# The expert-key stage of a two-layer attention and feed-forward kernel: order of its PSUM traffic, and smaller parts for the split expert weights

## The chip, the cores and the metric
One Trainium2 chip, one core. The metric is the device time in microseconds of one execution of the whole program. All times below are microseconds (us) unless marked ns.

## The reference, cut to what matters
Four sub-layers on x of 4 sequences, 512 tokens, 256 channels, each added to x after a layer norm:

1. cross attention, 16 heads of 16 channels, with a time bias of -0.1 |t - t'|;
2. a dense feed-forward of 1024 channels plus product-key experts;
3. cross attention with relu on q, k and v, no bias;
4. eight experts of 512 channels with gelu, two chosen per token.

The change lies in the second (the "expert-key stage"), and in how the weights of the fourth are prepared during the first:

```python
q = einsum('btd,ed->bte', h, W_q); sim = einsum('pbthn,hkpn->pbthk', q, keys)   # 4 heads, 2 halves, 64 keys
sx, sy = top_k(sim, 8)
scores, pk = top_k(sx[:, None] + sy[None, :], 8)            # 8 of 64 pairs per head
w = silu(einsum('btd,bthkd->bthk', h, down_embed[indices]) * softmax(scores))
experts_states = einsum('bthk,bthkd->btd', w, up_embed[indices])
dense = silu(h @ W_up.T) @ W_down.T                          # 256 -> 1024 -> 256
```

## The kernel before, in words
Each engine has its own program, and semaphores order them. PSUM is one tile `ps` of 8 banks of 128 x 512 floats. Three parts matter.

**Attention 0** (0 to about 375 us) runs 64 units U (4 sequences x 4 head groups x 4 key blocks). In a unit TensorE makes four scores for the row maxima (L1002, VectorE reduces them at L1335), four scores by key (L1016), and the value products of the unit before (L1033); ScalarE takes the exp (L773); GpSimd multiplies the near-diagonal part (`near_bias`, L611) before the values may use it. Maxima of a head group are turned (L1050), copied (L1346) and carried by SyncE from `m_sb` into `sq` (`load_max`, L443), where the first scores by key of the group (units 48, 52, 56, 60 for the last sequence) wait for them. In units 3 and 19 GpSimd also does a layer norm (L558, then L568). Between near parts GpSimd splits each of the 8 experts' weights of sub-layer 4 into a high and a low part: `split_high` (L584), `split_low` (L590), `split_out` (L596, which stores them to HBM and asks for the raw weights of the expert after next, L603 and L604). Expert e's three parts run in units 5 + 7e, 6 + 7e and 7 + 7e. SyncE's program has, after its work for unit 56, `late_weights` (L483): it waits until all split weights are stored, then loads 4.9 MB of weights for the expert-key stage. After the last unit it queues the zeroing of 22 MB of `expert_rows` (L511).

**The expert-key stage** (375 to 793 us) works on 16 blocks n of 128 tokens, software-pipelined over steps s. The order of each engine's work in a step is written out by hand. Per block: `turn_norm` and `x_high`/`x_low` (once for two blocks: normed x turned to channels, in a high and a low part), `similarity` (L1115 with `wret`), `sim_copy`, `top8` on VectorE (L1558 to L1576, with L1560 and L1573 on SBUF), `turn_sim` (L1153), `turned_high` (L810) and `turned_low` (L1546), `hidden` (L1115 with `sk`: 1024 products of x with all experts, PSUM banks 0 and 1), and for each of 4 heads h: `logits` (L1174, 128 x 1024), `expand` (exp, L820), `mask` (L1584, keeps what is above the threshold), `times_hidden` (L1593), `weight_silu` (L835, in the next step). `norms8` (L1598 to L1603) makes the softmax sums, `clamped_pairs` (L635, L638, GpSimd) and `clamped_silu` (L840) a special expert. GpSimd's `add_heads` (L646) adds the four heads' 128 x 1024 weights. Three steps after its logits the block's summed weights are turned (`turn_weights`, L1181), copied, and multiplied with the up embeddings (`add_experts`, L1188). The dense feed-forward runs beside it: `ff_up` (L1115 with `ff1s`), `ff_silu`, `ff_down` (L1210). `add_pair` (L1611 to L1622) adds the results of two blocks to x. The copies of the front bank all go through `front_copy` (L791).

PSUM in this stage: banks 0 and 1 for `hidden`; banks 2 to 5 are two pairs, used in turn (`ring_free`) by a block's turned similarities and its four logits; bank 6 (`FRONT`) is used in the order of `front_order()` by x turned, similarities, summed weights turned, and the feed-forward in two halves; bank 7 sums the output. ScalarE's exp and silu are in different tables, so a step has two table loads.

The heads' weights live in buffers `wide`, of which head h has `KEEP[h]`: (3, 2, 2, 3).

**Attention 1** and the experts of sub-layer 4 follow (793 us to the end). Its q weights are scaled by `SCALE` on VectorE ahead of the expert-key stage (L1632).

## Time and profile before
| | us |
|---|---|
| median of 3 runs (1317.18 to 1319.8) | 1319.05 |
| the profiled execution | 1312.35 |
| its span, first to last instruction | 1310.5 |
| attention 0, to about | 375 |
| expert-key stage, its first logits to its last pair added | 397.2 to 793.1 |

The profile is of one execution. Busy time counts what an engine computes; instructions that only wait, branch or issue a DMA are not in it. "PE" is TensorE's matmul, "PEld" its weight load, "DVE" VectorE, "ACT" ScalarE, "POOL" GpSimd, "SPq" the DMA queue of SyncE. "[3.61 <-POOL pt L611]" behind a row means that the engine stood idle 3.61 us before it and that the named work of GpSimd ended the wait. Matmul ends are modelled and overlap, so a matmul row's length holds some latency at its end; GpSimd's spans are rough.

### The profile page before, as it was taken

Reading aid. Unit: us, or ns where it says so; the run is one execution under the profiler, and the core shown is the slowest. Engines: PE = TensorE matmul, PEld = TensorE weight load, DVE = VectorE, ACT = ScalarE, POOL = GpSimd, SP = SyncE. Lnnn points to the kernel's source line nnn. Section 1 sums busy time; section 2 is a strip of 40 time slices with the busy share of each in tenths; the row PEclk is TensorE's granted clock in tenths of the full one; section 3 lists DMA queues with packets and bytes.
Section 4 is the critical chain, followed back from the end, with each engine's and each line's share of the span. In section 5 each row is a group of like instructions: output and inputs, shape, how many; then the busy total and the mean of one; then the engine's idle time right before and its main releaser. Section 6 shows DMA issues by size and latency. Waiting matters only on the chain.

```text
span 1310.5 us, 16623 instructions
## 1 busy us (share of the span) xinstructions
PE 1060.7 (81%) x5420; PEld 653.2 (50%) x5420; DVE 809.9 (62%) x1941; ACT 661.0 (50%) x886; POOL 442.3 (34%) x342
## 2 busy tenths in 40 slices
PE   5797988988356788888888776999998985399992
PEld 3332333433134677767777664333333432288881
DVE  2755757677048878978888402677777773344443
ACT  2044645555344667566675632266656574155551
POOL 1327565566230434234343331011422143222220
PEclk9567989989679899999999988699988797599996
DMA  8836656651899800000000007436444334422226
GB/s 233 194 104 194 202 173 174 208 161 66 299 236 234 179 1 1 1 1 1 1 1 2 1 1 168 129 90 185 106 135 123 91 123 180 161 70 70 71 70 192
DMA packets 77801, 151.68 MB, mean 116 GB/s; under 512 B 8234, under 2 KB 48300, under 8 KB 76182
## 3 DMA queue, kind: packets, MB, share of 16 engines
q1 hardware_dynamic: 67446, 107.72, 31.8%
q0 software_dynamic: 9168, 42.12, 9.2%
q8 instruction: 46, 0.75, 0.3%
q10 hardware_dynamic: 1104, 0.79, 0.2%
q14 instruction: 37, 0.30, 0.1%
HBM read 73.88 MB, written 76.25 MB: 115 GB/s over the span
## 4 chain that ended last, share of the span: by engine, by line
PE 55%; DVE 12%; ACT 12%; issue 9%; POOL 6%; DMA 4%; SPq 1%; ACTq 0%; POOLq 0%; DVEq 0%
PE ps L1115 14%; PE ps L1033 6%; PE ps L1002 6%; DVE negmax L1335 6%; PE ps L981 6%; PE ps L1188 4%; PE ps L1016 3%; PE ps L1174 3%; PE ps L990 3%; PE ps L1210 2%; ACT moe_w L835 2%; POOL pt L611 2%; ACT pt L835 1%; POOL wst L590 1%; PE ps L1286 1%
## 5 line engine op out<-in xcount | busy, mean ns | idle before, releaser
L1335 DVE TENSOR_REDUCE negmax<-ps 128x1 f32<-128x512 f32 x512 | 320.9, 682 | 75.9 <-PE ps L1002 75.3
L773 ACT ACTIVATE pt<-ps 128x1024 f32<-128x1024 f32 x256 | 255.5, 1025 | 170.0 <-PE ps L1016 169.3
L1002 PE MATMUL ps<-sk,sq 56*128 56x512 f32 x512 | 174.6, 481 | 44.9 <-DVE negmax L1335 20.2
L1033 PE MATMUL ps<-pt,v_aug 128*32 128x512 f32 x1024 | 149.9, 660 | 19.7 <-POOL pt L611 18.7
L1016 PE MATMUL ps<-sq,sk 57*128 57x512 f32 x512 | 133.1, 511 | 21.0 <-DMA sq<-m_sb 19.8
L1002 PEld LDWEIGHTS ps<-sk,sq 56*128 56x128 f32 x512 | 78.2, 210 | 112.3 <-DVE negmax L1335 73.9
L611 POOL TENSOR_TENSOR pt<-pt,near 128x512 f32<-128x512 f32 x64 | 81.5, 1273 | 141.6 <-ACT pt L773 141.5
L1016 PEld LDWEIGHTS ps<-sq,sk 57*128 57x128 f32 x512 | 52.8, 201 | 121.8 <-issue 71.9
L686 POOL TENSOR_TENSOR x_tok<-x_tok,on 128x256 f32<-128x256 f32 x16 | 11.6, 725 | 228.5 <-DVE on L1355 228.5
L1174 PE MATMUL ps<-sel,hl 128*128 128x512 f32 x256 | 73.3, 420 | 6.7 <-DVE pt L1584 6.7
L708 POOL DMA_INDIRECT expert_out<-yo,dest x39 | 38.2, 979 | 117.3 <-ACT yo L921 89.3
L1115 PE MATMUL ps<-wexp,ghl 128*128 x468 | 67.2, 292 | 1.6 <-DVE ghl L1683 1.5
L1115 PE MATMUL ps<-wexp,xhl 128*128 x234 | 65.0, 414 | 1.5 <-DVE xhl L1679 1.5
L1683 DVE TENSOR_TENSOR ghl<-ps,ghl 128x512 fp32r<-128x512 f32 x39 | 27.0, 691 | 60.7 <-ACT ghl L914 60.7
L1210 PE MATMUL ps<-wff,on 128*128 128x256 f32 x256 | 63.6, 393 | 0.0
L635 POOL TENSOR_TENSOR wdown_e<-exm,ex 128x256 f32<-128x256 f32 x16 | 10.0, 626 | 158.6 <-DVEq L1605 158.6
L1188 PE MATMUL ps<-wup_e,xn 128*128 128x256 f32 x256 | 63.5, 385 | 0.0
L1115 PEld LDWEIGHTS ps<-wexp,ghl 128*128 128x128 f32 x468 | 58.9, 188 | 6.8 <-issue 2.2
L820 ACT ACTIVATE moe_w<-ps,negm 128x1024 f32<-128x1024 f32 x30 | 33.4, 1112 | 55.0 <-PE ps L1174 54.9
L1174 PEld LDWEIGHTS ps<-sel,hl 128*128 128x128 f32 x256 | 48.9, 193 | 18.3 <-DVE pt L1584 8.4
L1188 PEld LDWEIGHTS ps<-wup_e,xn 128*128 128x128 f32 x256 | 49.8, 195 | 8.3
L1033 PEld LDWEIGHTS ps<-pt,v_aug 128*32 128x32 f32 x1024 | 20.7, 111 | 61.3 <-issue 33.6
(251 smaller groups left out, 1996.6 us busy)
## 6 DMA issues: line engine op xcount, KB each, us to landing
expert_rows<-zero SPq DMA_DIRECT2D x3, 5586.0 KB, 58.2
qk_rows<-hl SPq DMA_DIRECT2D x32, 512.0 KB, 3.3
expert_weights_split<-wst POOLq DMA_DIRECT2D x8, 2048.0 KB, 8.6
sq<-qk_rows SPq DMA_DIRECT2D x64, 192.0 KB, 4.6
sk<-qk_rows SPq DMA_DIRECT2D x64, 192.0 KB, 5.3
qk_rows<-hl SPq DMA_DIRECT2D x32, 256.0 KB, 3.8
moe_w<-in_w POOLq DMA_DIRECT2D x16, 512.0 KB, 9.6
wexp<-expert_weights_split POOLq DMA_DIRECT2D x16, 512.0 KB, 5.0
```

Source lines behind the costliest of these rows:

```text
L611: pool.tensor_tensor(probs, probs, near[:].unsqueeze(1).broadcast_to([P, HG, P]), ALU.mult).then_inc(s_near, 1)
L773: act.activation(pt[:, 4 * (U % 2) + 2 * half:4 * (U % 2) + 2 * half + 2, :], ps[:, 2 + 2 * half:4 + 2 * half, :], ACT.Exp, scale=(BIAS, 1 ...
L835: act.activation(weight(n, h), weight(n, h), ACT.Silu, scale=rz[:, n % RING, h:h + 1]).then_inc(s_w4, 1)
L981: ins = pe.matmul(dst, w[L][:, part, i * P:(i + 1) * P], src[:, part, :], start=(part == 0), stop=(part == 1))
L1002: pe.matmul(ps[:, jbank(job), :], sq[r, pair, t * P:(t + 1) * P], sk[r, pair, :], start=True, stop=True).then_inc(s_job, 1)
L1016: ins = pe.matmul(ps[:, 2 + 2 * half + s, :], sk[r, pair, c * P:(c + 1) * P], sq[r, pair, :], start=True, stop=True)
L1033: ins = pe.matmul(ps[32 * j:32 * j + 32, OBANK, :], v_aug[:, b % 2, c, HG * g + j, :], pt[:, 4 * (U % 2) + j, :], start=(c == 0), stop=(c ...
L1115: ins = pe.matmul(dst, lhs(i), rhs(j), start=(first and i == j == 0), stop=(last and i == 1))
L1174: ins = pe.matmul(dst[:, j, :], turned[n % 2][:, i, h * P:(h + 1) * P], sel[:, NX * YK * j:NX * YK * (j + 1)], start=(i == 0), stop=(i == 1))
L1188: ins = pe.matmul(ps[:, YBANK, (n % 2) * D:(n % 2 + 1) * D], accT[:, c * P:(c + 1) * P], wup_e[:, c, :], start=False, stop=True, skip_grou ...
L1210: ins = pe.matmul(ps[:, YBANK, t * D:(t + 1) * D], ffh[:, 512 * i + 2 * P * r + P * t:512 * i + 2 * P * r + P * (t + 1)], wff2[:, f, :], s ...
L1335: dve.tensor_reduce(negmax[:, n % 2, col:col + 1], src, AX, ALU.max, negate=True).then_inc(s_jd, 1)
```

## The change
Attention 0:
- Expert e's split now has four parts in units 3 + 6e to 6 + 6e: high, low of the first half, low of the second half, out. `late_weights` stands after unit 53 instead of 56.

Expert-key stage:
- The turned similarities go through the front bank, and `front_order()` has them (`"T"`); the feed-forward goes through the bank pairs, all four of its 128-channel parts at once, in an order written down by `ring_order()`: the four logits of step s, then the feed-forward of block s - 2. `ff_silu` is one instruction of 128 x 1024.
- TensorE: `similarity(s + 2)` moves from the end of the step to between the third logits and the second part of `add_experts`; `turn_norm` to after the fourth logits; `ff_up` and then `turn_sim` close the step.
- ScalarE: `sim_copy` goes between the exps of heads 2 and 3, `x_high` behind them; the silus of heads 3 and 2, then the feed-forward's silu and `turned_high`, then the silus of heads 0 and 1.
- GpSimd: in step s it waits for the first mask of block s, then adds the heads of block s - 2 (before: of s - 1, without that wait), in the order 2, 0, 1, and only then does `clamped_pairs(s)`. Head 1 gets a third buffer (in `wff1`'s space).
- VectorE: `x_low` goes one step earlier, to between the products of heads 2 and 3.
- Start: both turns of x come before the first similarities. The scaling of the q weights of attention 1 is dropped, and `SCALE` is given to the exp there.

```diff
-RING, KEEP = 3, (3, 2, 2, 3)
+RING, KEEP = 3, (3, 3, 2, 3)
+def ring_order():
+    order = []
+    for s in range(NTL + 2):
+        if s < NTL:
+            order += [("S", s, h) for h in range(RH)]
+        if s >= 2:
+            order.append(("ff", s - 2, 0))
+    return order
@@ sync
-                    if L == 0 and U == 56:
+                    if L == 0 and U == 53:
                         late_weights()
@@ gpsimd
-                e, part = divmod(U - 5, 7)
-                if 0 <= e < ME and part < 3:
-                    (split_high, split_low, split_out)[part](e)
+                e, part = divmod(U - 3, 6)
+                if 0 <= e < ME:
+                    if part == 0:
+                        split_high(e)
+                    if part in (1, 2):
+                        split_low(e, part - 1)
+                    if part == 3:
+                        split_out(e)
-            for s in range(NTL + 1):
+            for s in range(NTL + 2):
+                if s < NTL:
+                    pool.wait_ge(s_pm, RH * s + 1)
+                if s >= 2:
+                    add_heads(s - 2)
                 if s < NTL:
                     clamped_pairs(s)
-                if s >= 1:
-                    add_heads(s - 1)
@@ scalar, one step
                     small_exp(s)
                     expand(s, 2)
-                    expand(s, 3)
-                if 0 <= s - 2 < NTL:
-                    ff_silu(s - 2, 0)
-                if s + 1 < NTL:
-                    turned_high(s + 1)
-                if 0 <= s - 2 < NTL:
-                    ff_silu(s - 2, 1)
-                if 0 <= s - 1 < NTL:
-                    weight_silu(s - 1, 3)
-                    weight_silu(s - 1, 1)
                 if s + 2 < NTL:
                     sim_copy(s + 2)
+                if s < NTL:
+                    expand(s, 3)
                 if s % 2 and (s + 3) // 2 < NTL // 2:
                     x_high((s + 3) // 2)
                 if 0 <= s - 1 < NTL:
+                    weight_silu(s - 1, 3)
                     weight_silu(s - 1, 2)
+                if 0 <= s - 2 < NTL:
+                    ff_silu(s - 2)
+                if s + 1 < NTL:
+                    turned_high(s + 1)
+                if 0 <= s - 1 < NTL:
                     weight_silu(s - 1, 0)
+                    weight_silu(s - 1, 1)
                     clamped_silu(s - 1)
@@ tensor, one step
                     logits(n, 2)
+                if s + 2 < NTL:
+                    similarity(s + 2)
...
                     logits(n, 3)
+                if s % 2 and (s + 3) // 2 < NTL // 2:
+                    turn_norm((s + 3) // 2)
                 if 0 <= y < NTL:
                     add_experts(y, range(6, EC))
                 if 0 <= s - 2 < NTL:
-                    ff_up(s - 2, 0)
+                    ff_up(s - 2)
                 if s + 1 < NTL:
                     turn_sim(s + 1)
-                if 0 <= s - 2 < NTL:
-                    ff_up(s - 2, 1)
-                if s + 2 < NTL:
-                    similarity(s + 2)
-                if s % 2 and (s + 3) // 2 < NTL // 2:
-                    turn_norm((s + 3) // 2)
+            def pair_free(item):
+                i = pairs[item]
+                if i >= 2:
+                    kind, m, h = order4[i - 2]
+                    pe.wait_ge(*((s_fs, m + 1) if kind == "ff" else (s_pm, RH * m + h + 1)))
+                return ps[:, 2 + 2 * (i % 2):4 + 2 * (i % 2), :]
@@ vector, start
-            dve.wait_ge(s_late, 16 * 8)
-            own(dve.tensor_scalar(wq[1][:], wq[1][:], SCALE, None, ALU.mult))
```

## Rows read from the trace of the kernel before

**Rows 1.** The page's first part: busy time, share of the span, instructions.
```profile
PE 1060.7 (81%) x5420; PEld 653.2 (50%) x5420; DVE 809.9 (62%) x1941; ACT 661.0 (50%) x886; POOL 442.3 (34%) x342
```
**Rows 2.** Windows: stretch, length, then PE, PEld, DVE, ACT, POOL busy, clock, DMA, GB/s.
```profile
334.80:353.40 18.60, 0.04 (x6) 0.02 (x2) 0.00 (x0) 0.00 (x0) 1.15 (x1) 0.59 0.86 301
...
443.80:740.00 296.20, 254.85 (x1317) 213.34 (x1317) 240.47 (x569) 193.81 (x248) 110.25 (x65) 0.99 0.03 6
740.00:793.10 53.10, 39.07 (x202) 33.13 (x200) 9.36 (x18) 22.97 (x31) 15.88 (x9) 0.94 0.07 8
...
559.45:606.04 46.59, 39.96 (x208) 33.42 (x209) 38.82 (x95) 30.52 (x40) 17.00 (x10) 1.00 0.00 1
```
**Rows 3.** Timeline of SyncE's DMA queue: start, length, what is issued.
```profile
298.46 16.23 SPq L443 DMA_DIRECT2D sq<-m_sb  x4
336.41 0.91 SPq L483 DMA_DIRECT2D wff<-in_ff  x2
...
345.40 2.14 SPq L443 DMA_DIRECT2D sq<-m_sb  x2
```
**Rows 4.** The page's DMA issues: count, KB each, median us to landing.
```profile
expert_weights_split<-wst POOLq DMA_DIRECT2D x8, 2048.0 KB, 8.6
```
**Rows 5.** Timeline of TensorE around the hole.
```profile
325.83 0.73 PE L1016 MATMUL ps<-sq,sk 57*128 57x512 f32 x4
...
353.38 1.22 PE L1016 MATMUL ps<-sq,sk 57*128 57x512 f32 x4 [18.56 <-DMA sq<-m_sb]
```
**Rows 6.** Timeline of ScalarE and TensorE over one step of the expert-key stage.
```profile
585.69 1.14 ACT L835 ACTIVATE w_first<-w_first,rz 128x1024 f32<-128x1024 f32 x1
586.73 1.14 ACT L835 ACTIVATE moe_w<-moe_w,rz 128x1024 f32<-128x1024 f32 x1
...
590.94 1.28 ACT L820 ACT_TABLE_LOAD   x1
...
592.23 1.11 ACT L820 ACTIVATE pt<-ps,negm 128x1024 f32<-128x1024 f32 x1
...
594.24 0.60 ACT L791 ACTIVATE xn<-ps 128x512 f32<-128x512 f32 x1
...
594.89 0.66 PE L1181 MATMUL ps<-ident,moe_w 128*128 128x128 f32 x4 [0.67 <-ACT xn L791]
...
600.45 1.27 PE L1174 MATMUL ps<-sel,hl 128*128 128x512 f32 x4
...
601.76 1.12 ACT L820 ACTIVATE moe_w<-ps,negm 128x1024 f32<-128x1024 f32 x1 [1.11 <-PE ps L1174]
```
**Rows 7.** Timeline of GpSimd in attention 0: norm, high part, near part, low part.
```profile
94.62 4.83 POOL L558 TENSOR_SCALAR xn<-x_tok,mv,rstd 128x256 f32<-128x256 f32 x4
...
110.07 1.89 POOL L584 CAST wst<-moe_w 128x2048 fp32r<-128x2048 f32 x1 [2.58 <-DMA moe_w<-in_w]
...
294.70 1.29 POOL L611 TENSOR_TENSOR pt<-pt,near 128x512 f32<-128x512 f32 x1
...
322.78 4.56 POOL L590 TENSOR_TENSOR wst<-moe_w,wst 128x2048 fp32r<-128x2048 f32 x1
```
**Rows 8.** Waits of TensorE, 40 to 375: total, times, longest.
```profile
PE ps L1033 <- POOL pt L611: 18.7, 8, 4.9
```
**Rows 9.** Timeline of GpSimd and VectorE at the stage's start.
```profile
374.75 4.50 POOL L625 TENSOR_TENSOR sk<-wdown_e,sk 128x2048 fp32r<-128x2048 f32 x1 [8.66 <-ACT sk L853]
...
375.75 3.78 DVE L1632 TENSOR_SCALAR wq<-wq 128x512 f32<-128x512 f32 x1
```
**Rows 10.** Groups by line, 559.45 to 606.04: busy us, mean ns, idle before.
```profile
L1560 DVE TENSOR_TENSOR wdown_e<-sxy 128x256 f32<-128x256 f32 x2 | 3.1, 1528 | 0.1
L1573 DVE TENSOR_TENSOR wdown_e<-wdown_e,v 128x256 f32<-128x256 f32 x2 | 3.0, 1500 | 0.1
```
**Rows 11.** One line's instructions over the run: ns shortest, median, longest.
```profile
L1560 DVE TENSOR_TENSOR wdown_e<-sxy x16: 425/1036/2039, 389.0 to 705.4; 128x256 f32<-128x256 f32 x16
```
**Rows 12.** Timeline of VectorE and GpSimd: a mask beside a sum.
```profile
731.25 1.28 DVE L1584 SCALAR_TENSOR_TENSOR pt<-ps,thr,pt 128x1024 f32<-128x1024 f32 x1 [4.88 <-ACT pt L820]
731.33 2.36 POOL L646 TENSOR_TENSOR w_first<-w_first,pt 128x1024 f32<-128x1024 f32 x1
```

More of the change, by code:

```diff
@@ L171, in front_order @@
 def front_order():
-    order = [("xt", 0, 0), ("sim", 0, 0), ("sim", 1, 0), ("xt", 1, 0)]
+    order = [("xt", 0, 0), ("xt", 1, 0), ("sim", 0, 0), ("sim", 1, 0), ("T", 0, 0)]
     for s in range(NTL + 3):
@@ L176, in front_order @@
             order += [("at", s - 3, 0), ("at", s - 3, 1)]
-        if 0 <= s - 2 < NTL:
-            order += [("ff", s - 2, 0), ("ff", s - 2, 1)]
         if s + 2 < NTL:
@@ L182, in front_order @@
             order.append(("xt", (s + 3) // 2, 0))
+        if s + 1 < NTL:
+            order.append(("T", s + 1, 0))
+    return order
[6 more added lines that the diff above has]
+            order.append(("ff", s - 2, 0))
     return order
@@ L365, in build @@
         order6 = front_order()
+        pairs = {item: n for n, item in enumerate(ring_order())}
+        order4 = ring_order()
+        pair_of = lambda item: ps[:, 2 + 2 * (pairs[item] % 2):4 + 2 * (pairs[item] % 2), :].rearrange("p a t -> p (a t)")
         s_x = [sem(f"x_in{b}") for b in range(B)]
@@ L513, in _ @@
             sp.wait_ge(s_hd, NTL)
-            sp.wait_ge(s_front, front["ff", NTL - 1, 1] + 1)
+            sp.wait_ge(s_f, NTL)
             const_rows(1)
@@ L640, in add_heads @@
             def add_heads(n):
-                for i, h in enumerate((1, 2, 0)):
+                for i, h in enumerate((2, 0, 1)):
                     pool.wait_ge(s_w4, RH * n + i + 2)
@@ L794, in x_high @@
                 if p >= 4:
-                    act.wait_ge(s_front, front["ff", 2 * (p - 4) + 1, 1] + 1)
+                    act.wait_ge(s_f, 2 * (p - 4) + 2)
                     act.wait_ge(s_hd, 2 * (p - 4) + 2)
@@ L800, in sim_copy @@
                 if n >= 2:
-                    act.wait_ge(s_T, n - 1)
+                    act.wait_ge(s_front, front["T", n - 2, 0] + 1)
                     act.wait_ge(s_top, n - 1)
@@ L805, in turned_high @@
             def turned_high(n):
-                act.wait_ge(s_T, n + 1)
                 if n >= 2:
                     act.wait_ge(s_S, RH * (n - 1))
-                r = 2 + 2 * (5 * n % 2)
-                act.copy(turned[n % 2][:, 0], ps[:, r, :]).then_inc(s_th, 1)
+                front_copy(turned[n % 2][:, 0], ("T", n, 0))
             def expand(n, h):
-                i = 1 + 5 * n + h
                 act.wait_ge(s_S, RH * n + h + 1)
@@ L1220, in _ @@
             turn_norm(0)
+            turn_norm(1)
             similarity(0)
+            similarity(1)
             turn_sim(0)
-            similarity(1)
-            turn_norm(1)
             for s in range(NTL + 3):
@@ L1543, in turned_low @@
             def turned_low(n):
-                dve.wait_ge(s_th, n + 1)
-                r = 2 + 2 * (5 * n % 2)
-                dve.tensor_tensor(turned[n % 2][:, 1], ps[:, r, :], turned[n % 2][:, 0].bitcast(F32), ALU.subtract).then_inc(s_tl, 1)
+                dve.wait_ge(s_fe, front["T", n, 0] + 1)
+                dve.tensor_tensor(turned[n % 2][:, 1], ps[:, FRONT, :], turned[n % 2][:, 0].bitcast(F32), ALU.subtract).then_inc(s_tl, 1)
             def top8(n):
@@ L1666, in _ @@
                     times_hidden(n, 2)
+                if s % 2 and (s + 3) // 2 < NTL // 2:
+                    x_low((s + 3) // 2)
+                if n < NTL:
                     times_hidden(n, 3)
```

86 lines of the change are left out of this document (43 added, 43 removed).

## The prediction
> **What bounds the kernel now.** The page's first line says that TensorE is busy 81% of the span and every other engine less [rows 1]; an average over stages doesn't say what a stage waits for, so I read the windows view next [rows 2]. In 334.8 to 353.4 no engine computes: 18.6 us are lost. From 443.8 to 740.0, the body of the expert-key stage, TensorE is busy 86% and VectorE 81%: neither is full, so an order of work holds it. The chain of waits repeats there every two steps; the window of two steps is 46.59 us, one step 23.3.
>
> The hole: the timeline of SyncE's queue [rows 3] shows the loads of the last group of row maxima (L443, `sq<-m_sb`) at 345.40, behind the late weights (L483) that start at 336.41, because SyncE waits there for the last split expert weights to be stored; that store has a median of 8.6 from issue to landing [rows 4]. TensorE [rows 5] waits 18.56 for those maxima, until 353.38.
>
> The body: I follow one step through the timeline [rows 6], from its last logits to the next ones. ScalarE turns it around: exp at 601.76, silus, a table load at 590.94 in the step before, the two exps, the copy at 594.24; TensorE has it from 594.89 to the last logits at 600.45. ScalarE also waits twice within it, because the feed-forward goes through the one front bank in two halves with a silu each (the first ends near 606.0).
>
> **Part 1, expert weights.** Expert 7 is now sent in unit 48, not 56. In [rows 7] the near multiply of unit 48 starts at 294.70 and ends at 296. With 8.6 for the store the late weights can start at 304.6. Their issue lasts 9.0 (336.41 to 345.40 [rows 3]), to 313.6. The next maxima are asked for at about 313.4 in the trace (they are the second pair of the row 298.46, which is 16.23 long), so SyncE is free when it is asked. Behind the weights they land some 17 after the weights' start (336.41 to 353.38), at 321.6. TensorE wants them in unit 56, at 325.83 [rows 5]: 4 us are left. The last group, asked for near 330, finds an empty queue. **18.6 saved**; if the store or the queue takes some us more, a new wait of up to 6 takes its place: 13 to 20 (above 18.6, because TensorE starts again cold after the hole: clock 0.59 in it [rows 2]).
>
> GpSimd's low half of 4.56 [rows 7] becomes two of 2.28. TensorE takes about 4.3 for a unit (from the norm of unit 3 at 94.6 to the hole at 334.8, 56 units) and the near multiply 1.3, so a piece of 2.3 fits beside it and one of 4.5 does not. TensorE waited for this multiply 18.7 in eight waits [rows 8]. What is late next: in unit 3 the norm (4.83), the bias add (2.3), the loads (3.3), their landing (2.58) and the high part (1.89) now stand in one row, 14.9, instead of 7.2 and 7.7 with two multiplies between. I work out that the values of unit 9 come some 4 later; in unit 19 the norm is rid of the high part beside it (2 to 3 won), and the low parts give about 4. Net **2 saved**, -4 to 7.
>
> **Part 2, start of the stage.** The scaling of `wq` on VectorE becomes a constant of ScalarE's exp, which costs nothing. Its row is 3.78 long [rows 9] for 512 columns and it ended 0.3 after GpSimd's 4.50, which began at 374.75: it was held by GpSimd. What is late next may be the norm behind it, held till the same 379.3; then 0.5 is won, and 3.6 if the norm is not held. Against this, a second turn, copy, low part and norm go ahead of the first similarity, about 3 on the path, while the first copy of similarities no longer stands behind the square root, 1. I take **1 saved**, -1 to 4.
>
> The Trainium skill (SBUF — State Buffer, section Who interferes with whom) says that a DVE `tensor_scalar` can enter a mode that contends with GpSimd, and that an instruction with two SBUF inputs contends with a GpSimd one that reads SBUF. The 3.78 agrees with such a lock. By that rule the norm, too, is held, and this part gives under 1.
>
> **Part 3, the steps.** The new circle from [rows 6], counted from the issue of a step's last logits:
> - to the start of its exp 1.31 (600.45 to 601.76), exp 1.12, table load 1.28;
> - two weight silus at a pitch of 1.04 (585.69, 586.73), 2.08; the feed-forward silu, now one of the same size, 1.04 (its 24 matmuls end about 5.1 after the start, ScalarE comes at 5.8, so both waits of before are gone); the copy of the turned similarities 0.5;
> - two more silus 2.08, the clamped one 0.61, table load 1.29, two exps 2.01 (592.23 to 594.24), copy and turn-around 0.65. Together 13.97.
> - TensorE from there: 5.56 as now (594.89 to 600.45) and the similarity put in between, six matmuls, 1.4: 6.96.
>
> A step takes 20.9. Odd steps add a copy (0.5) and a turn (0.4): 21.8.
>
> Beside it lies VectorE, 19.4 a step now [rows 2]. The sums now run after the first mask, 3 x 2.4 = 7.2. Before, they ran beside the top-8 block, where L1560 and L1573 average 1.53 and 1.50 [rows 10]; L1560's shortest is 0.43 and its longest 2.04 [rows 11]. Laid out from start to start the block loses 2.2 in one step and 3.4 in the next, so VectorE needs 19.4 - 2.8 = 16.6. Does the new company hold the masks? At 731.25 a mask takes 1.28 with a GpSimd sum beside it from 731.33 [rows 12], as without: no. It may hold the small products of `norms8`, which read SBUF twice like L1573: in odd steps the masks come late (first mask ends 17.4 after the circle's start, behind `add_pair`, 2.6, and the norm, 0.8), the sums end at 24.9, and `norms8`, due at 23.5, waits 1.4. Last mask, two products and low part pass it on to the next hidden block, which has 1.1 to spare: 0.3 reaches the circle. The new wait of exp 2 for the first sum (its buffer has two turns): in even steps the first mask ends at 13.7, the sum at 16.1, and the exp is due at 18.6, so it is free; in odd ones it is 0.8 late, where the mask behind it has that slack. The held sums are wanted a step after they end, and `clamped_pairs`, moved behind them, has its reader a step away.
>
> Mean (20.9 + 22.1) / 2 = 21.5 against 23.3: 1.8 x 12.7 steps (296.2 / 23.3) = **22.9 saved**. TensorE's own floor is 39.96 / 2 = 20.0, so the circle still binds. Bounds: 22.5 if VectorE's path decides (10 saved), 20.9 throughout (30).
>
> Before 443.8 one top-8 block loses its company: **2 saved**, -2 to 4. The tail, 53.1 from 740.0 [rows 2]: laid out the same way it is 48.6 (the last feed-forward blocks in one piece each, but two weight silus queue behind a feed-forward silu that waits for TensorE): **4.5 saved**, 0 to 8.
>
> **Sum.** 18.6 + 2 + 1 + 22.9 + 2 + 4.5 = 51.0. The profiled execution took 1312.35 (span 1310.5 and 1.85 around it), so its like would take 1261.35. The median of the three runs is 1319.05, 6.7 above it; I take the saving from the median: **1268.0 us**.
>
> **Rivals.**
> A. *The circle is not what binds the body.* VectorE's chain (turned low, pair add, top-8, masks) or the pair banks hold a step at 23. For it: VectorE at 81%, and only 1.1 spare in odd steps; against it: the 2.8 it gets back. The stage gives 4 instead of 22.9: 1286.9. Chance 0.16.
> B. *The maxima are caught again.* 5 MB stand ahead of a small load that TensorE wants 4 us after. Were the last store 13 later, 9 of the hole come back: 1277. For it: 17 us of queue. Against it: the margin of about a unit. Chance 0.08.
> C. *Slower.* One mechanism: GpSimd's sums and the masks exclude each other. VectorE then needs 16.6 + 7.2 = 23.8, and with the waits for ScalarE that it can't avoid (about 2.6) a step takes 26.4: 3.1 x 12.7 = 39 lost against 28.1 won elsewhere: 1330. The whole is slower from a step of 25.5 on. Against it stands the mask at 731.25. Chance 0.04.
> D. *Better*: masks and sums keep clear, all steps take 20.9, the splits give their 7: 1255. Chance 0.12.
> E. *It does nothing*, other waits take all of it: 1319. Chance 0.03.
>
> **How the numbers follow.** The forecast's own case has 0.57. Its terms' bounds, added as squares, give 11 below and 16 above: 1257 to 1284. To leave out no more than 2 in 10 I reach towards A and D: 1251 to 1290. Faster by over 0.2% (2.6 us, about what can be told from no change): forecast, A, B and D, 0.93; same 0.03 (E); slower 0.04 (C).
>
> **What would show it.** No wait of many us for `m_sb` near 334, the late weights issued near 305; one longer hole in unit 3 on GpSimd's account; two steps in about 43 us, with no ScalarE wait between halves of a feed-forward; L1560 and L1573 at 0.43, masks still 1.28; `norms8` products stretched in odd steps. The forecast is wrong if two steps take over 45, or if the hole of part 1 only moves.

## The result and the profile after

| | before | after |
|---|---|---|
| median of the timed runs | 1318.32 us | 1263.27 us (1258.83 to 1268.79, 4 runs) |
| ratio, 95% interval | | 0.9585 (0.9562 to 0.9608) |
| span of the profiled execution | 1310.5 us | 1257.0 us |

The kernel is 55 us faster; 1268.0 was forecast and the time lies inside 1251 to 1290. In a second series of the changed kernel (below) two of six runs, 1358.07 and 3112.83 us, were disturbed and are left out. The page's first part, after, against [rows 1]: TensorE does the same 5420 matmuls, VectorE is busy 31.8 us less.

```profile
PE 1048.3 (83%) x5420; PEld 651.6 (52%) x5420; DVE 778.1 (62%) x1940; ACT 659.1 (52%) x870; POOL 443.4 (35%) x350
```

Where the 53.5 us between the two spans went is read from the same events in both traces: the first logits of the stage, those of step 3, the last logits of step 15, the last `add_pair`. Three rows of the timeline of before (TensorE, VectorE; its last logits are at 740.00, where a window of [rows 2] begins), and four of after:

```profile
397.18 1.97 PE L1174 MATMUL ps<-sel,hl 128*128 128x512 f32 x8
...
450.41 1.99 PE L1174 MATMUL ps<-sel,hl 128*128 128x512 f32 x8
...
793.06 0.69 DVE L1611 TENSOR_TENSOR x_tok<-ps,x_tok 128x512 f32<-128x512 f32 x1 [21.43 <-PE ps L1188]
```
```profile
373.26 1.98 PE L1198 MATMUL ps<-sel,hl 128*128 128x512 f32 x8
...
427.60 2.01 PE L1198 MATMUL ps<-sel,hl 128*128 128x512 f32 x8
...
691.88 1.28 PE L1198 MATMUL ps<-sel,hl 128*128 128x512 f32 x4
...
735.47 0.69 DVE L1631 TENSOR_TENSOR x_tok<-ps,x_tok 128x512 f32<-128x512 f32 x1 [19.43 <-PE ps L1212]
```

| stretch | before | after | saved | forecast |
|---|---|---|---|---|
| to the first logits (parts 1 and 2) | 397.18 | 373.26 | 23.9 | 21.6 |
| first logits to step 3 (ramp) | 53.23 | 54.34 | -1.1 | 2 |
| step 3 to the last logits (body) | 289.59 | 264.28 | 25.3 | 22.9 |
| last logits to the last pair (tail) | 53.06 | 43.59 | 9.5 | 4.5 |
| the rest of the kernel | 517.4 | 521.5 | -4.1 | 0 |

These are one trace each, and they scatter. A second trace of the changed kernel has 372.16, 59.47, 269.21, 43.36 and 522.0 in these rows: between two executions of the same kernel the ramp and the body each differ by 5 us, and the tail does not. TensorE's mean granted clock in the ramp was 0.91 in the first trace and 0.80 in the second.

The hole is gone. SyncE's queue of after, where [rows 3] showed the late weights at 336.41 and the last maxima at 345.40: the weights are issued at 299.42, and the maxima that units 56 and 60 want (L458) follow from 308.53.

```profile
299.42 0.91 SPq L498 DMA_DIRECT2D wff<-in_ff  x2
...
308.53 15.96 SPq L458 DMA_DIRECT2D sq<-m_sb  x4
```

The waits of TensorE from 40 to 375 (total, times, longest) now hold 1.8 us for `m_sb`. The waits for the near multiply, 18.7 in [rows 8], are not fewer:

```profile
PE ps L1053 <- POOL pt L626: 19.9, 9, 11.3
...
PE ps L1036 <- DMA sq<-m_sb: 1.8, 3, 1.1
```

The 11.3 is the wait for the near multiply that follows unit 3's long row. GpSimd's timeline there shows norm, bias, loads and high part in one row, 14.9 us from 92.14 to 107.02, before the near multiply that TensorE wants:

```profile
92.14 4.83 POOL L573 TENSOR_SCALAR xn<-x_tok,mv,rstd 128x256 f32<-128x256 f32 x4
97.05 2.34 POOL L583 TENSOR_TENSOR x_tok<-x_tok,bo_bc 128x1024 f32<-128x1024 f32 x1
...
105.16 1.89 POOL L599 CAST wst<-moe_w 128x2048 fp32r<-128x2048 f32 x1 [2.59 <-DMA moe_w<-in_w]
107.02 1.25 POOL L626 TENSOR_TENSOR pt<-pt,near 128x512 f32<-128x512 f32 x1
```

The body: the windows view of two steps, after (length, PE, PEld, DVE, ACT, POOL busy, clock). 46.59 of [rows 2] became 42.78, VectorE's busy time fell from 38.82 to 34.43:

```profile
546.70:589.48 42.78, 39.07 (x211) 33.47 (x209) 34.43 (x95) 30.32 (x37) 17.02 (x11) 1.00 0.00 1
```

ScalarE's timeline of one step, against [rows 6]. The step's last logits start at 546.70, those of the next at 567.48, 20.8 later. From the exp at 548.01 to the copy at 559.91 no row has a wait, and the feed-forward has a single silu (L850, 552.54) of one microsecond where two stood with a wait each:

```profile
548.01 1.12 ACT L841 ACTIVATE wff<-ps,negm 128x1024 f32<-128x1024 f32 x1 [1.53 <-PE ps L1198]
549.14 1.28 ACT L856 ACT_TABLE_LOAD   x1
550.44 1.16 ACT L856 ACTIVATE w_first<-w_first,rz 128x1024 f32<-128x1024 f32 x1
...
552.54 1.00 ACT L850 ACTIVATE on<-ps 128x1024 f32<-128x1024 f32 x1
553.44 0.58 ACT L813 ACTIVATE hl<-ps 128x512 fp32r<-128x512 f32 x1
...
557.90 2.12 ACT L841 ACTIVATE pt<-ps,negm 128x1024 f32<-128x1024 f32 x2
559.91 0.60 ACT L813 ACTIVATE xn<-ps 128x512 f32<-128x512 f32 x1
```

VectorE's lines over the whole run (ns shortest, median, longest). The first product of the top-8 block (L1582) is at 424 where [rows 11] had 1036, the masks (L1605) stay at 1283, and the small product of `norms8` (L1619) has a new longest of 1750:

```profile
L1582 DVE TENSOR_TENSOR wdown_e<-sxy x16: 424/424/1072, 365.8 to 662.1; 128x256 f32<-128x256 f32 x16
...
L1605 DVE SCALAR_TENSOR_TENSOR moe_w<-ps,thr,moe_w x26: 1273/1283/1285, 379.2 to 692.1; 128x1024 f32<-128x1024 f32 x26
...
L1619 DVE TENSOR_TENSOR exm<-ex,ixg x16: 179/182/1750, 381.7 to 694.5; 128x32 f32<-128x32 f32 x16
```

### The profile page after: what moved, and what is told of

Same layout as the page of the kernel before. It is cut to its first block, busy times and chain, and to the rows that moved or that the text cites. A ratio compares the mean times of both kernels' runs of the same rounds, so it can differ in the third digit from the quotient of the medians.

```text
span 1257.0 us, 16614 instructions
## 1 busy us (share of the span) xinstructions
PE 1048.3 (83%) x5420; PEld 651.6 (52%) x5420; DVE 778.1 (62%) x1940; ACT 659.1 (52%) x870; POOL 443.4 (35%) x350
## 4 chain that ended last, share of the span: by engine, by line
PE 55%; DVE 20%; ACT 7%; issue 7%; POOL 5%; DMA 4%; SPq 1%; ACTq 0%; DVEq 0%; POOLq 0%
PE ps L1135 14%; PE ps L1053 7%; PE ps L1022 7%; DVE negmax L1358 6%; PE ps L1001 6%; PE ps L1036 4%; PE ps L1010 3%; PE ps L1235 3%; PE ps L1198 3%; PE ps L1212 2%; DMA sq<-m_sb 2%; PE ps L1062 1%; PE ps L1309 1%; DVE moe_w L1613 1%; POOL pt L626 1%
## 5 line engine op out<-in xcount | busy, mean ns | idle before, releaser
L795 ACT ACTIVATE pt<-ps 128x1024 f32<-128x1024 f32 x256 | 255.8, 1025 | 157.0 <-PE ps L1036 150.3
L1022 PE MATMUL ps<-sk,sq 56*128 56x512 f32 x512 | 175.0, 478 | 48.3 <-DVE negmax L1358 21.2
L1053 PE MATMUL ps<-pt,v_aug 128*32 128x512 f32 x1024 | 146.9, 648 | 20.8 <-POOL pt L626 19.9
L708 POOL TENSOR_TENSOR x_tok<-x_tok,on 128x256 f32<-128x256 f32 x16 | 11.6, 725 | 234.0 <-DVE on L1378 234.0
L666 POOL TENSOR_TENSOR w_first<-w_first,moe_w 128x1024 f32<-128x1024 f32 x16 | 38.1, 2379 | 108.1 <-DVE pt L1605 107.3
L1605 DVE SCALAR_TENSOR_TENSOR moe_w<-ps,thr,moe_w 128x1024 f32<-128x1024 f32 x26 | 33.3, 1280 | 37.7 <-ACT moe_w L841 37.6
L841 ACT ACTIVATE moe_w<-ps,negm 128x1024 f32<-128x1024 f32 x26 | 28.9, 1112 | 49.1 <-PE ps L1198 27.9
```

The lines of the kernel that those rows point to most:

```text
L666: pool.tensor_tensor(weight(n, 3), weight(n, 3), weight(n, h), ALU.add).then_inc(s_sum, 1)
L795: act.activation(pt[:, 4 * (U % 2) + 2 * half:4 * (U % 2) + 2 * half + 2, :], ps[:, 2 + 2 * half:4 + 2 * half, :], ACT.Exp, scale=(BIAS, S ...
L1022: pe.matmul(ps[:, jbank(job), :], sq[r, pair, t * P:(t + 1) * P], sk[r, pair, :], start=True, stop=True).then_inc(s_job, 1)
L1053: ins = pe.matmul(ps[32 * j:32 * j + 32, OBANK, :], v_aug[:, b % 2, c, HG * g + j, :], pt[:, 4 * (U % 2) + j, :], start=(c == 0), stop=(c ...
```

## Experiments

The time from the last logits of step 3 to those of step 14, eleven steps, is the measure of the body below: 255.4 before (460.8 to 716.2) and 234.0 in this trace of after (438.5 to 672.5). A step counts as odd when it is the one in which the next tokens' normalised low part is made (20.8 us from 546.70 to 567.48 is an even one, 22.0 to 589.48 an odd one).

### Part 1 alone

```diff
-                    if L == 0 and U == 56:
+                    if L == 0 and U == 53:
...
-                e, part = divmod(U - 5, 7)
-                if 0 <= e < ME and part < 3:
-                    (split_high, split_low, split_out)[part](e)
+                e, part = divmod(U - 3, 6)
...
+                    if part in (1, 2):
+                        split_low(e, part - 1)
...
```


> The kernel before with part 1 alone: the split of the expert weights in four parts from unit 3 on, every 6 units, and the late weights after unit 53. The stage marks of the two profiles put 22.3 us of the gain ahead of the end of attention 0. If that is part 1's, this kernel takes 1318.3 - 22.3 = 1296, and two steps of the expert-key stage stay at 46.6. If part of the gain in attention 0 came from elsewhere (the run's clock), it takes 1299 to 1305.

Measured: 1291.36 us (1285.72 to 1298.86) against 1317.36; ratio 0.9812 (0.9745 to 0.9879), a saving of 24.8 with some 9 to either side. By the marks of its trace the first logits come at 373.65 instead of 397.18, 23.5 earlier; the body takes 255.4, as before, and two steps take 46.59. So the marks add up: part 1 brings its 22 to 24 and nothing behind it. The steadiest mark is the time from the first scores by key of unit 47 to those of unit 63: 73.2 in the traces of the kernel before and of the one with the held sums alone (below), 51.1 here and 51.0 in the first trace of the changed kernel, so 22.1 saved.

### The late weights where they were

```diff
-                    if L == 0 and U == 53:
+                    if L == 0 and U == 56:
```


> The changed kernel with the late weights back after unit 56. Theory 1 (the hole came from the late store of expert 7, not from the place of the loads): the store is done by about 299, the weights are then issued after the third pair of maxima, near 310, and have landed before the last pair is wanted: 1263 to 1265. Theory 2 (the place counts): the last pair of maxima stands behind 5 MB again, asked for at 323 and landed near 329 where TensorE wants it at 330: 1266 to 1275.

Measured: 1263.36 us; ratio 0.9586 (0.9535 to 0.9638), the same as the changed kernel. SyncE's queue in it: the maxima of units 52 and 56 are issued ahead of the weights, and the weights follow at once, without a wait for the store. The last maxima (unit 60's) are issued at 321.90, behind the weights, and TensorE does not wait for them either.

```profile
293.38 14.43 SPq L458 DMA_DIRECT2D sq<-m_sb  x4
307.92 0.91 SPq L498 DMA_DIRECT2D wff<-in_ff  x2
```

With the early store the place of the weights in the queue makes no difference: what caught the maxima was the late store. The old pacing with the weights at unit 53 can't be tried: SyncE would wait there for a store of unit 56, whose scores need maxima loaded behind it.

### Splits one unit later

```diff
-                e, part = divmod(U - 3, 6)
+                e, part = divmod(U - 4, 6)
```


> The changed kernel with the split parts one unit later (unit 4 + 6e and on), so that the first high part, with its loads, doesn't stand in the unit of the norm. Theory: the wait of 11.3 for GpSimd near 108 falls to about 4 and a second of about 2 comes: 4 to 5 us faster than the changed kernel, 1259. Rival: TensorE makes up for it within some units anyway, or unit 19 (norm beside store and loads) takes it back: 1262 to 1264.

Measured: 1266.84 us; ratio 0.9612 (0.9561 to 0.9663): no gain. The long wait in unit 3 did shrink (the longest for a near multiply is 5.2 instead of 11.3), but at the other end rival B came true in small. SyncE's queue, then TensorE:

```profile
306.61 0.91 SPq L498 DMA_DIRECT2D wff<-in_ff  x2
```
```profile
323.22 0.50 PE L1036 MATMUL ps<-sq,sk 57*128 57x512 f32 x2 [3.24 <-DMA sq<-m_sb]
```

The weights wait for the last store, are issued 7.2 later than in the changed kernel, and stand in front of the maxima: TensorE waits 3.24 for them in unit 56. This also tells how much slack the changed kernel has: here the maxima are issued at 316.67 and used 6.55 later, there they are issued at 308.53 and used at 316.03, so about 0.9 us was left. The last logits of the first step come at 389.1, 9.8 later than in the changed kernel; 3.24 of this is that wait, 3.4 was there by unit 47 (288.65 against 285.29), which lies within what traces of the same pacing scatter by (283.5 to 289.8), and the rest was not taken apart. The expectation of 1259 was wrong since it looked at unit 3 alone.

### Held sums alone

```diff
-RING, KEEP = 3, (3, 2, 2, 3)
+RING, KEEP = 3, (3, 3, 2, 3)
...
-                for i, h in enumerate((1, 2, 0)):
+                for i, h in enumerate((2, 1, 0)):
...
-            for s in range(NTL + 1):
+            for s in range(NTL + 2):
+                if s < NTL:
+                    pool.wait_ge(s_pm, RH * s + 1)
+                if s >= 2:
+                    add_heads(s - 2)
                 if s < NTL:
                     clamped_pairs(s)
-                if s >= 1:
-                    add_heads(s - 1)
...
```


> The kernel before with the held sums alone: GpSimd waits for the first mask and adds the heads of block s - 2, in the order 2, 1, 0, with a third buffer for head 1. Theory 1 (the chain through ScalarE and TensorE binds, and it is as long as before): top-8 is freed of its company, and the time stays within 4 us of 1318. Theory 2 (VectorE's work binds): 2.8 a step are won, two steps take 41 to 43, the kernel 1284.

Measured: 1316.59 us; ratio 0.9997 (0.9971 to 1.0023). The top-8 product is at 424 (median) and VectorE is 5.5 us less busy in two steps than in [rows 2], but the two steps take the same 46.60:

```profile
549.50:596.10 46.60, 39.98 (x211) 33.43 (x209) 33.27 (x94) 30.54 (x40) 16.95 (x11) 1.00 0.00 1
```

The body takes 255.4 (456.4 to 711.8), to the tenth that of before. VectorE did not bind the body: rival A, as far as it names VectorE, is out for the kernel before.

### Everything but the held sums

```diff
-            for s in range(NTL + 2):
-                if s < NTL:
-                    pool.wait_ge(s_pm, RH * s + 1)
-                if s >= 2:
-                    add_heads(s - 2)
+            for s in range(NTL + 1):
                 if s < NTL:
                     clamped_pairs(s)
+                if s >= 1:
+                    add_heads(s - 1)
```


> The changed kernel with GpSimd's order of before: clamped pairs of step s, then the sums of block s - 1, no wait for the mask. Theory 1 (the sums' company lengthens the top-8 block, and in odd steps VectorE passes that on): the two SBUF tensor operations of top-8 go back to 1.5 on average, two steps go from 42.8 to 44 to 46, the kernel takes 1270 to 1282. Theory 2 (the chain through ScalarE alone binds, VectorE has room): two steps stay at 42.8, within 3 us of 1263.

Measured: 1273.65 us; ratio 0.9688 (0.9631 to 0.9745), 10 us more than the changed kernel. Two steps take 47.3, more than the 44 to 46 expected. Windows of two steps, and VectorE's lines (ns shortest, median, longest), where the product into `x_tok` takes 482 (median) in the changed kernel:

```profile
549.70:597.00 47.30, 41.15 (x211) 34.50 (x209) 39.72 (x95) 30.32 (x37) 17.06 (x10) 0.96 0.00 1
```
```profile
L1633 DVE SCALAR_TENSOR_TENSOR x_tok<-last_up,wc,x_tok x16: 478/2570/2600, 465.5 to 751.6; 128x256 f32<-128x256 f32 x16
...
L1580 DVE TENSOR_TENSOR wdown_e<-sxy x16: 424/1553/2161, 364.1 to 677.1; 128x256 f32<-128x256 f32 x16
```

One of two steps takes 21.3, the other (which the changed kernel does in 20.8) 26.0, and the body 251.9 (435.6 to 687.4). So neither half does much alone:

| body, 11 steps | sums as before | sums held |
|---|---|---|
| the other edits not made | 255.4 | 255.4 |
| the other edits made | 251.9 | 234.0 (238.9 in a second trace, below) |

The circle of ScalarE and TensorE hid VectorE's slowness; once it is shortened, VectorE's path with the stretched operations sets every second step, and the held sums remove that. Which of the other edits shortened the circle, and by how much each, no run takes apart: the order of TensorE and ScalarE, the traffic of the banks and the single silu were changed together.

### A copy more on ScalarE, a sum more on VectorE

Two kernels, each the changed one with one instruction of 128x512 more in each step from 3; its result is read by nobody.

```diff
+                    if s >= 3:
+                        act.activation(wff1[:, 1, 0:512], wff1[:, 1, 512:FF], ACT.Copy)
```


> The changed kernel with one more copy of 128 x 512 on ScalarE behind the fourth exp, in steps 3 to 15 (result unused). A copy costs ScalarE 0.5 from start to start. Theory 1 (ScalarE's chain binds): 0.5 in each even step and 0 to 0.5 in odd ones, where ScalarE waits up to 0.5 for the turned similarities: 3 to 6.5 us slower than the changed kernel, 1266 to 1270. Theory 2 (VectorE's chain binds both steps): within 1 us of 1263.


```diff
+                if 3 <= s < NTL:
+                    dve.tensor_tensor(wff1[:, 1, 0:512], wff1[:, 1, 512:FF], wff1[:, 1, 512:FF], ALU.add)
```


> The changed kernel with one more sum of 128 x 512 on VectorE ahead of top-8, in steps 3 to 15 (result unused), 0.6 from start to start. Theory 1 (ScalarE's chain binds even steps, VectorE's tail leaks into odd ones only): 0 in even and 0.6 in odd steps, 3 to 4 us slower, 1267. Theory 2 (VectorE's chain binds both steps): 0.6 in each, 8 us slower, 1271. Theory 3 (ScalarE's chain alone): 1263.

Measured: 1267.54 us, ratio 0.962 (0.956 to 0.968), for the copy; 1272.91 us, ratio 0.9659 (0.9604 to 0.9713), for the sum. By the last logits of each step in the traces, even steps are 21.3 with the copy and 20.8 to 21.2 with the sum: ScalarE's circle sets them, and the copy of 0.5 goes straight through. Odd steps from 5 on are 22.0 to 23.6 with the copy, as without it (22.0 to 23.7 in the two traces of the changed kernel), and 23.6 to 25.3 with the sum: VectorE's path sets those. The theory that ScalarE's chain sets all steps holds for the even ones alone. The sum was to cost 3 to 4 us and cost about 10: each of its odd steps is long, and the next rows show what else than the 0.6 of the sum lies in a long one.

### A third buffer for head 2

```diff
-RING, KEEP = 3, (3, 3, 2, 3)
+RING, KEEP = 3, (3, 3, 3, 3)
...
```


> The changed kernel with a third buffer for head 2, so that its exp no longer waits for GpSimd's first sum (0.8 in odd steps). Theory 1 (that wait is hidden: the norms' product waits for the third sum in any case): within 1 us of 1263. Theory 2 (the wait is on the path): 0.8 in six odd steps, 5 us faster, 1258.

Measured: 1264.44 us; ratio 0.9597 (0.9544 to 0.9649), no difference. The wait of exp 2 for the first sum (3.82 at 565.90 in the changed kernel) is gone and nothing moved: it was hidden. But in this trace two steps take 44.3, not 42.8, and one row shows why. TensorE at the end of an odd step, of the changed kernel and of this one, then windows of this one:

```profile
575.78 3.00 PE L1135 MATMUL ps<-sk,xs 128*128 128x512 f32 x12 [0.55 <-DVE w_first L1613]
```
```profile
577.13 4.56 PE L1135 MATMUL ps<-sk,xs 128*128 128x512 f32 x12 [0.55 <-DVE w_first L1613]
```
```profile
573.30:577.10 3.80, 1.60 (x13) 1.19 (x11) 3.69 (x4) 3.27 (x4) 0.91 (x2) 1.00 0.00 0
577.10:581.50 4.40, 4.37 (x12) 3.56 (x13) 4.08 (x26) 4.03 (x6) 0.00 (x0) 0.61 0.01 4
```

TensorE computes for 1.60 of 3.80 us, with waits of 1.69 and 0.55 between, the second for VectorE, and then the granted clock is 0.61 on average for 4.40 us (1.00 is 2.4 GHz, 0.5 is 1.2 GHz): the same 12 matmuls take 1.56 longer.

### The changed kernel again, with and without spare work for TensorE

> The changed kernel itself once more, as the reference for the two that follow. Two of its relatives (late56, three_bufs) showed two steps in 44.3 to 44.4 where the first trace of the changed kernel shows 42.8; the difference is one stretch of 12 matmuls in odd steps, 3.0 at a granted clock of 1.00 or 4.4 at 0.61. Theory 1 (chance decides it, the same kernel shows both): this trace has some steps of 22.0 and some of 23.5, and the runs spread over 1258 to 1269. Theory 2 (the first trace is the rule for this kernel): all odd steps but one at 22.0.


```diff
+                if s % 2 and 3 <= s and s + 1 < NTL:
+                    spare = pair_free(("S", s + 1, 0))
+                    for k in range(KC):
+                        products(spare[:, 0, :], lambda i: xst[s // 2 % 4][:, i, k, 0:P], lambda j: wret[:, j, k, :], k == 0, k == KC - 1)
```


> The changed kernel with six spare matmuls (128x512) in each odd step from 3, put into a free pair bank while TensorE waits there, before the similarities are turned; their result is overwritten unread. Theory 1 (TensorE's idle of 2.2 in 3.8 us is why its clock falls, and the slow 12 matmuls are the whole difference between steps of 22.0 and 23.5): all odd steps take 22.0, the 12 matmuls 3.0 at clock 1.00; against the changed kernel in the same series 0 to 7 us faster, by how many of its steps are slow, about 1258 to 1261. Theory 2 (the clock falls for other reasons, or the spare work is itself in the way): steps of 23.5 stay, 1263 or more.

Measured, in one series: 1261.67 us (median of four runs, 1258.69 to 1267.98), ratio 0.9585 (0.9547 to 0.9622), and 1259.45 us (1254.90 to 1262.52), ratio 0.9581 (0.9552 to 0.961), with the spare matmuls (six runs). The second trace of the changed kernel has two steps of 44.40 at a clock of 0.96, where the first has 42.78 at 1.00. With the spare work all odd steps from 5 on take 22.0 to 22.3 (two steps: 42.80 at 1.00), although TensorE is busy for 1.6 us more than in the first trace (40.69 against 39.07):

```profile
552.50:596.90 44.40, 40.68 (x211) 34.69 (x209) 34.54 (x95) 30.33 (x37) 17.15 (x11) 0.96 0.00 1
```
```profile
548.20:591.00 42.80, 40.69 (x217) 34.51 (x215) 34.50 (x95) 30.32 (x37) 17.06 (x11) 1.00 0.00 1
...
573.40:577.20 3.80, 3.24 (x19) 2.27 (x17) 3.76 (x4) 3.24 (x4) 0.96 (x2) 1.00 0.00 0
```

The traces show theory 1: the same kernel has both lengths of odd step, and filling the idle stretch (3.24 busy of 3.80 instead of 1.60) keeps the clock. The idle stretch is needed for the loss but is not enough for it: in the first trace it was there and the clock stayed. The two medians alone don't separate the kernels.

### `norms8` ahead of the masks

```diff
                 if n < NTL:
+                    norms8(n)
                     mask(n, 0)
                     mask(n, 1)
...
-                    norms8(n)
                     mask(n, 3)
```


> VectorE does the two small products of norms8 before the first two masks of a step, not after the third. Theory 1 (in odd steps VectorE's path sets the length: the product is held 1.4 to 2.1 by GpSimd's third sum, and TensorE's next 12 matmuls wait for the masks and products behind it): that product takes 0.18 in every step, the odd steps shrink from 22.0 or 23.5 to 21.3 (ScalarE's 20.8 and its extra copy of 0.5), the even ones stay at 20.8, TensorE no longer idles long enough to lose its clock; 1252 to 1259. Theory 2 (something else sets the odd step): 1262 to 1266 as before it, though the product is no longer held.

Measured: 1266.70 us; ratio 0.9634 (0.9599 to 0.967), no gain or a small loss. The mechanism is as theory 1 has it: the small product takes 180 to 183 ns in all 16 steps, TensorE's 12 matmuls 3.00, odd steps 21.6, and the body 233.6 against 238.9 in the reference of the same series. But for the first blocks and for every even block (whose masks lie at the end of an odd step) the exps that `norms8` reads are not done yet, and the masks behind `norms8` now wait for them, 2.15 in block 0 and 3.4 in block 10:

```profile
377.86 0.19 DVE L1618 TENSOR_REDUCE zz<-ex 128x4 f32<-128x32 f32 x1 [2.15 <-ACT ex L844]
...
589.75 0.19 DVE L1618 TENSOR_REDUCE zz<-ex 128x4 f32<-128x32 f32 x1 [3.41 <-ACT ex L844]
```

Even steps are 21.1 instead of 20.8 (this is in the 233.6). No such wait is in them: there `norms8` itself, about 0.9 from its first row to its last, now stands between the norm and the first mask. From the first logits to the last ones of step 3 it is 0.8 longer and from those of step 14 to the last pair 1.2, which is 2 of the 5.3 that the body gives. In this trace the other 3 are lost outside the stage, which starts 2.2 later and is followed by 0.9 more than in the reference; whether the median shows no gain for this reason is not shown.

### Together

```diff
-RING, KEEP = 3, (3, 3, 2, 3)
+RING, KEEP = 3, (3, 3, 3, 3)
...
+                    if n % 2 and n >= 3:
+                        norms8(n)
                     mask(n, 0)
...
-                    norms8(n)
+                    if n % 2 == 0 or n < 3:
+                        norms8(n)
                     mask(n, 3)
-                    times_hidden(n, 2)
                 if s % 2 and (s + 3) // 2 < NTL // 2:
                     x_low((s + 3) // 2)
                 if n < NTL:
+                    times_hidden(n, 2)
                     times_hidden(n, 3)
```


> What the last runs point to, together: the products of norms8 go before the first masks in odd steps from 3 alone (there the small exp they need is already done; in even steps it is not, and norms_up held the masks for it), the third buffer of head 2 as in three_bufs, and the low part of the normalised tokens one product earlier. Theory 1 (the odd steps hang on VectorE's path behind the held product, the even ones on ScalarE's circle): even steps 20.8 as in the changed kernel, odd ones 21.3 to 21.6 with the 12 matmuls at full clock, the ramp as in the changed kernel; against its 22.0 to 23.5 in six odd steps that is 3 to 13 less: 1252 to 1259. Theory 2 (what norms_up lost was not only the wait of the masks in even steps): 1262 or more.

Measured: 1252.25 us (1246.18 to 1257.68) against 1309.71; ratio 0.9551 (0.9516 to 0.9586). The body takes 231.5 (445.9 to 677.4) and two steps 42.40 at a clock of 1.00. Odd steps are 21.3, as expected; even ones are 21.1 where 20.8 was expected, since `norms8` stands ahead of the first mask there as in the run before:

```profile
552.00:594.40 42.40, 39.39 (x210) 33.34 (x209) 33.33 (x95) 30.32 (x37) 16.97 (x11) 1.00 0.01 1
```

Its ratio is 0.0034 below that of the changed kernel, 4.5 us, and the intervals overlap; the body in the trace is 2.5 and 7.4 shorter than in the two traces of the changed kernel. Part of its lower median is that the kernel before was quicker in this series too.

## Why the prediction was right, and where it was off

The mechanisms of the hole and of the even steps were right, and the body's size nearly so; in odd steps VectorE decides, not ScalarE. That the sum came within 5 us of the median is in part luck: in the table of stretches the five misses add up to 17 us without their signs and to 2.5 with them.

- *Part 1, the hole.* Right, mechanism and size. Store, late weights (estimated 304.6, issued 299.42), maxima in time: 18.6 of the 23.9; TensorE's longest wait for `m_sb` fell from 18.56 [rows 5] to 1.1. The weights were earlier than estimated for two reasons: unit 48's near multiply came 3.2 earlier (below), and they left 6.7 after the store's issue at 292.73, not 8.6. The margin was misread. The prediction has TensorE want the maxima of unit 56 at 325.83 [rows 5], landed at 321.6, with 4 us left; but that row is unit 57 (four scores by key to a unit, 512 in the two attentions), and unit 56 starts at this one, in the kernel before:

```profile
321.57 0.50 PE L1016 MATMUL ps<-sq,sk 57*128 57x512 f32 x2
```

  With the weights at 304.6 nothing would have been left. They came 5.2 earlier, unit 56 came 5.5 earlier too (316.03), and about 0.9 was left: no wait, but that was luck and not the margin laid out. With the splits one unit later it is used up.
- *Part 1, pacing.* The long row in unit 3 came as laid out (14.9), the longest wait for a near multiply rose from 4.9 to 11.3, and the sum of these waits from 18.7 to 19.9. The near multiply of unit 48, at 294.70 in [rows 7], is at 291.50, but these 3.2 are not the pacing's: the kernel with the held sums alone, which has the old pacing, has it at 291.27. What is steady lies behind unit 47. From there to unit 59 the old pacing takes 43.05 (43.06 with the held sums alone) and the new 40.54, 2.5 saved where I had 2, and from unit 59 to 63, where the hole was, 30.14 became 10.48. GpSimd's timeline:

```profile
291.50 1.27 POOL L626 TENSOR_TENSOR pt<-pt,near 128x512 f32<-128x512 f32 x1
292.73 0.61 POOL L611 DMA_DIRECT2D expert_weights_split<-wst  x1
```

- *Part 2.* The norm was held, as allowed for: two pieces took 1.36 (the first alone 1.04) where the run's median of one is 0.41.

```profile
350.13 4.51 POOL L645 TENSOR_TENSOR sk<-wdown_e,sk 128x2048 fp32r<-128x2048 f32 x1 [9.95 <-ACT sk L874]
```
```profile
353.75 1.36 DVE L1559 TENSOR_SCALAR oT<-x_tok,mv,rstd 128x256 f32<-128x256 f32 x2
```

  The first piece ended about when GpSimd's 4.51 did (354.6). How much part 2 gave is not shown: the first logits come at 373.65 with part 1 alone and at 373.26 with all, 0.4 apart, and from the first scores of unit 63 to them it is 36.3 with part 1 alone, 37.0 and 34.0 in the two traces of the changed kernel. By the rule of the Trainium skill (SBUF — State Buffer, section Who interferes with whom) a `tensor_scalar` can be held in this way; this row agrees.
- *The circle in even steps.* 20.9 forecast, 20.8 measured, and a copy more on ScalarE lengthens them by its 0.5: this step of the working is shown.
- *Odd steps.* 22.1 forecast, 22.0 or 23.5 measured. I had ScalarE's two more operations setting them, with VectorE 0.3 over; the two extra-work runs show that it is VectorE. Its rows: the `norms8` product is held by GpSimd's third sum, as forecast (1.4), and everything behind it comes late, until TensorE's 12 matmuls wait for the last product.

```profile
569.38 0.17 DVE L1618 TENSOR_REDUCE zz<-ex 128x4 f32<-128x32 f32 x1
569.47 1.43 DVE L1619 TENSOR_TENSOR exm<-ex,ixg 128x32 f32<-128x32 f32 x1
...
573.82 0.68 DVE L1563 TENSOR_TENSOR hl<-ps,hl 128x512 fp32r<-128x512 f32 x1
574.42 1.22 DVE L1613 TENSOR_TENSOR w_first<-ps,w_first 128x1024 f32<-128x1024 f32 x1
```

  The rule of the Trainium skill (SBUF — State Buffer, section Who interferes with whom) on instructions with two SBUF inputs agrees with this row, and with the masks, which have one input in PSUM and were not held. What I did not think of is the clock: 1.5 of the step in some executions. It is why the body of the same kernel is 4.9 longer in its second trace.
- *Body.* 25.3 measured against 22.9. Over steps 3 to 14 the mean step went from 255.4 / 11 = 23.2 to 234.0 / 11 = 21.3 in this trace and 238.9 / 11 = 21.7 in the second, against 23.3 and 21.5 forecast. The gain per step was off by 0.1 to 0.3. What the table has beyond the 22.9 comes mostly from the last step: up to the last logits of step 15 it takes 19.4 in both traces where it took 23.8 before, and the forecast had priced all steps alike.
- *Held sums.* I forecast no cost for the masks beside a sum: right (1283 before and after). I gave the relief of VectorE no price of its own, because the circle binds; on its own that is right (0.9997), but taken away from the changed kernel it costs 10 us. `add_pair` takes 2.7 in the first trace (554.66 to 557.33) where my layout had 2.6.
- *Ramp.* 2 saved forecast, 1.1 lost, and 6.2 lost in the second trace. This term was guessed from one top-8 block. Its last step shows what it left out: it takes 24.7 (21.9 before), the `norms8` product is held there too (1.45), and TensorE waits for VectorE's last product and then does its 12 matmuls in 4.58 instead of 3.00:

```profile
423.18 4.58 PE L1135 MATMUL ps<-sk,xs 128*128 128x512 f32 x12 [3.23 <-DVE wff L1613]
```

  The rest was not taken apart.
- *Tail.* The term that was sized worst: 4.5 forecast, 9.5 measured. The last three steps in blocks, from one first feed-forward matmul to the next: before 741.78, 760.27, 778.83 and the end at 793.06; after 693.67, 707.31, 723.49 and the end at 735.47. That is 4.9, 2.4 and 2.3 saved. I had let the silus behind the feed-forward silu eat about half of this. ScalarE's rows show it mostly in the second block (710.57: two silus, 711.49, stand between it and the copy at 715.68, for which TensorE waits 2.67); in the first, two silus went ahead of the feed-forward silu, while TensorE made its 24 matmuls, and TensorE waits 1.06 for the copy at 701.20.

```profile
697.72 1.00 ACT L850 ACTIVATE on<-ps 128x1024 f32<-128x1024 f32 x1
...
701.20 0.58 ACT L813 ACTIVATE xn<-ps 128x512 f32<-128x512 f32 x1
...
710.57 1.02 ACT L850 ACTIVATE on<-ps 128x1024 f32<-128x1024 f32 x1 [5.32 <-PE ps L1135]
711.49 2.17 ACT L856 ACTIVATE pt<-pt,rz 128x1024 f32<-128x1024 f32 x2
...
715.68 0.58 ACT L813 ACTIVATE xn<-ps 128x512 f32<-128x512 f32 x1
```
- *The rest.* 4.1 lost, with nothing changed in it but the scale given to the exp of attention 1 (the 256 exps of both attentions have a mean of 1025 ns before and after). From the last pair to the end the kernel with held sums alone takes 521.9 and the one with part 1 alone 519.9, and of those built on the changed kernel the one with the spare matmuls takes 517.5 and the last one 515.1: the loss lies within the scatter between executions.
- *Rivals.* A is out for the kernel before, as far as VectorE goes, and half true after: VectorE's path sets the odd steps, at 22 to 23.5, not 23 for all. The pair banks, its other half, had no run of their own; they are used five times a step before and after, and the steps shrank. B did not happen, but does one unit further on. C did not happen (masks at 1283). D's 20.9 in every step is nearly reached by the last experiment (21.1 and 21.3).

## What to carry to other kernels

Two engines' paths of nearly the same length hide each other's faults: relieving the one that doesn't bind gave nothing by itself, and 10 us once the other was shortened, so an edit's worth has to be read from the kernel it will live in. When a step is rebuilt, follow each of its instructions to who is beside it on GpSimd, and check that what an operation reads is ready before it is moved ahead of others. A slack in a queue is part of the design, and the row that it is read from decides it: 4 us on paper were 0.9 in the trace, and moving the last store by one unit used them up. Compare a difference of a few microseconds between two traces with that between two traces of one kernel before giving it a cause.

## What was not expected of the hardware

The granted clock of TensorE fell within the body, which looks full: after 1.60 us of work in 3.80 the next 12 matmuls ran at 0.61 for 4.40 us and took 4.56 instead of 3.00. In four traces all odd steps from 5 to 11 are long by this (23.4 to 23.7), in the first trace of the changed kernel one is, for the same instructions; with 3.24 of 3.80 busy every odd step from 5 on stayed at 22.0 to 22.3. In the ramp, too, the clock decides microseconds: the same stretch took 54.34 at 0.91 and 59.47 at 0.80. What sets which of the two an execution gets is open. GpSimd's sums held a VectorE product of 128x32 values for 1.42 to 2.12 us instead of 0.18, and the product into `x_tok`, of 128x256 values, for 2.57 instead of 0.48 (median, with the sums early): the small one was held for up to 2.12 all the same.
